# A mixture-of-experts tail on one core: the 7 busiest of 15 routed experts stay dense, the other 8 run on 64 gathered tokens in fp32 in two column groups

## The reference

```python
E = 16; K = 4                      # 16 routed experts, 4 for each token; D = 512, H = 1365
gate_out = x @ gate_w + routing_bias
top_v, top_i = jax.lax.top_k(gate_out, K)
chosen = jax.nn.one_hot(top_i, E, dtype=x.dtype).sum(axis=-2)
weights = jax.nn.softmax(jnp.where(chosen > 0, gate_out, NEG), axis=-1) * chosen
out = _swiglu(x, sw1, sw2, sw3)    # the shared expert
for e in range(E):
    out = out + _swiglu(x, w1[e], w2[e], w3[e]) * weights[..., e:e + 1]
# _swiglu(x, w1, w2, w3): a = x @ w1; return a * sigmoid(a) * (x @ w2) @ w3
```

## Time and profile before

| | before |
|---|---|
| time, median of 3 | 535.69 us |
| the profiled execution | 535.71 us |
| its span | 533.7 us |
| mean granted TensorE clock | 0.994 |
| PE busy | 522.6 us |
| DVE busy | 425.1 us |
| ACT busy | 337.2 us |
| moved by DMA | 190.11 MB |

### The profile page before, as it was taken

The page is one execution under the profiler, slowest core; times in us unless marked ns, Lnnn a source line. Parts: engine busy times, 40 slices in busy tenths (PEclk is TensorE's granted clock), DMA queues, the critical chain, the costliest instruction groups (busy, mean ns, idle before and its releaser), DMA issues.

```text
span 533.7 us, 7582 instructions
## 1 busy us (share of the span) xinstructions
PE 522.6 (98%) x2672; PEld 406.9 (76%) x2672; DVE 425.1 (80%) x426; ACT 337.2 (63%) x324; POOL 8.9 (2%) x40
## 2 busy tenths in 40 slices
PE   8999799999999999999999999999999999999998
PEld 4665335467878888888888888888888888888886
DVE  6724610167899989889898998989998988989796
ACT  1100100158787878788786877877787877778573
POOL 2000000011000000000000000000000000000000
PEclk9988999999999999999999999999999999999999
DMA  8999999999999999999989999899999999999331
GB/s 338 422 421 421 421 421 422 417 409 416 414 404 414 372 375 348 351 394 337 404 284 380 374 344 384 320 381 339 368 358 356 345 341 395 340 369 350 123 108 70
DMA packets 37032, 190.11 MB, mean 356 GB/s; under 512 B 4090, under 2 KB 4474, under 8 KB 31636
## 3 DMA queue, kind: packets, MB, share of 16 engines
q1 hardware_dynamic: 36816, 189.70, 92.0%
q10 hardware_dynamic: 196, 0.14, 0.1%
HBM read 189.56 MB, written 0.26 MB: 356 GB/s over the span
## 4 chain that ended last, share of the span: by engine, by line
PE 91%; DVE 7%; ACT 1%; issue 1%; DMA 1%; POOL 0%; DVEq 0%; ACTq 0%; POOLq 0%
PE ps L1572 29%; PE ps L1610 23%; PE ps L1576 14%; PE ps L1594 4%; PE ps L1221 3%; PE ps L1385 3%; DVE s_lo L891 2%; PE ps L1414 1%; PE ps L1402 1%; PE ps L1214 1%; PE ps L1283 1%; PE ps L1299 1%; DVE s_lo L903 1%; PE ps L1273 1%; PE ps L1287 1%; PE ps L1545 1%
## 5 line engine op out<-in xcount | busy, mean ns | idle before, releaser
L891 DVE TENSOR_TENSOR s_lo<-w_raw,s_hi 128x1365 fp32r<-128x1365 f32 x136 | 209.1, 1579 | 16.0 <-ACT s_hi L657 15.6
L657 ACT CAST s_hi<-w_raw 128x1365 fp32r<-128x1365 f32 x136 | 180.4, 1337 | 26.3 <-PE ps L1576 13.1
L1572 PE MATMUL ps<-s_hi,xT_hi 128*128 128x512 f32 (+1 forms) x408 | 153.7, 377 | 0.3 <-DVE s_lo L891 0.3
L1572 PE MATMUL ps<-s_lo,xT_hi 128*128 128x512 f32 (+1 forms) x408 | 149.7, 369 | 0.0
L1576 PE MATMUL ps<-s_hi,xT_lo 128*128 128x512 f32 (+1 forms) x408 | 106.6, 369 | 0.0
L903 DVE TENSOR_TENSOR s_lo<-w_raw,s_hi 128x1536 fp32r<-128x1536 f32 x68 | 105.8, 1578 | 0.0
L669 ACT CAST s_hi<-w_raw 128x1536 fp32r<-128x1536 f32 x68 | 90.8, 1343 | 21.4 <-PE ps L1576 18.3
L1572 PEld LDWEIGHTS ps<-s_hi,xT_hi 128*128 128x128 f32 x408 | 76.6, 188 | 17.0 <-DVE s_lo L891 0.5
L1572 PEld LDWEIGHTS ps<-s_lo,xT_hi 128*128 128x128 f32 x408 | 77.0, 189 | 12.5
L1576 PEld LDWEIGHTS ps<-s_hi,xT_lo 128*128 128x128 f32 x408 | 72.7, 189 | 6.0
L1610 PE MATMUL ps<-s_hi,hT_hi 128*128 128x512 f32 (+1 forms) x180 | 72.8, 404 | 0.2 <-DVE hT_lo L1097 0.2
(11 more groups left out here) (249 smaller groups left out, 305.5 us busy)
## 6 DMA issues: line engine op xcount, KB each, us to landing
w_raw<-in_w SPq DMA_DIRECT2D x128, 682.5 KB, 6.2
w_raw<-in_w SPq DMA_DIRECT2D x51, 768.0 KB, 6.1
w_set<-in_w SPq DMA_DIRECT2D x31, 1024.0 KB, 24.5
w_raw<-in_w SPq DMA_DIRECT2D x12, 512.0 KB, 5.8
w_raw<-in_sw SPq DMA_DIRECT2D x8, 682.5 KB, 15.6
wk_sb<-in_wk SPq DMA_DIRECT2D x2, 1024.0 KB, 16.6
wq_sb<-in_wq SPq DMA_DIRECT2D x2, 1024.0 KB, 16.0
gcn_sb<-in_gcn_w SPq DMA_DIRECT2D x2, 1024.0 KB, 13.1
```

The source lines that it names most:

```text
L657: a.copy(s_hi[pair][:, 0:F1], raw[:]).then_inc(hi_ready, 1)
L891: v.tensor_tensor(s_lo[pair][:, 0:F1], raw[:], s_hi[pair][:, 0:F1].bitcast(F32), ALU.subtract).then_inc(lo_ready, 1)
L1572: mm(bank(i + c0 // D)[:, 0:n], xT_hi[:, k], w[:, c0:c0 + n], start=(k == 0 and w is hi), stop=False)
```

## The change

Routed expert 0 stays at its place as a dense body. The other 15 are sorted on the chip by how many tokens chose them. Since 128 tokens choose 4 each, at most 7 experts can have more than 64 tokens. The 7 busiest run densely as before (bodies D), the other 8 as sparse bodies (S), in the order `KINDS`:

- A 0/1 matrix `hots` picks the tokens of each sparse expert: four matmuls gather x into `exS`, 64 rows an expert (`gather_few`). `spread`, made of the gates, later adds the 64 rows of the result back to the 128 (`spread_few`, `add_few`).
- A sparse body multiplies the raw fp32 weights as they are, without a split. The 64 tokens take 64 of the 128 columns of the array; the other 64 get the same tokens and the second half of the expert's 1365 features (683 each). A raw tile is free again when TensorE has used it (`raw_used`).
- SyncE reads each body's expert number from a table made by `plan_order`, and waits for that table before the loads of body 2.
- There are five pairs instead of six, all loops are written out, and w3 is laid out by single experts (dense: 11 tiles each; sparse: the two halves, 6 tiles each, the last of 43 rows).

```diff
-JOIN = 3
-JOINED = NE // JOIN * JOIN - (NE % JOIN == 0) * JOIN
-assert NE - JOINED == 2
-ALONE = JOIN
-CARRY = [F1 * j // P * P for j in range(1, JOIN)]
-CARRY = [0] + [F1 * j - c for j, c in zip(range(1, JOIN), CARRY)] + [0]
-TILES = [(F1 + CARRY[j]) // P for j in range(JOIN - 1)] + [-(-(F1 + CARRY[JOIN - 1]) // P), FT]
-LAST_ROWS = [P] * (JOIN - 1) + [F1 + CARRY[JOIN - 1] - (TILES[JOIN - 1] - 1) * P, F1 - (FT - 1) * P]
-H_COLS = max(FT * P, F1 + max(CARRY))
-DOWN = [[(0, 3), (3, 3), (6, 3), (9, n - 9)] for n in TILES]
-HT_CHUNK = [[(0, 4), (4, 4), (8, n - 8)] for n in TILES]
-W3_UNITS = len(DOWN[0])
-UNITS = 2 * KT + W3_UNITS
+LAST_ROWS = F1 - (FT - 1) * P
+DOWN = [(0, 3), (3, 3), (6, 3), (9, FT - 9)]
+HT_CHUNK = [(0, 4), (4, 4), (8, FT - 8)]
+W3_UNITS = len(DOWN)
+FEW = P // 2
+HALVES = P // FEW
+CW = -(-F1 // HALVES)
+S_TILES = -(-CW // P)
+S_LAST = CW - (S_TILES - 1) * P
+S_LOADED = -(-S_LAST // 16) * 16
+S_CHUNK = [(0, 512), (512, CW - 512)]
+S_HT = [(0, 4), (4, S_TILES - 4)]
+BUSY = P * K1 // (FEW + 1)
+KINDS = "DD" + "SD" * 5 + "SSDSD"
+FULL = [m for m in range(NE) if KINDS[m] == "D"]
+SPARSE = [m for m in range(NE) if KINDS[m] == "S"]
...
-PAIRS_N = 6
+PAIRS_N = 5
...
+    unit_of, few_of = {}, {}
+    for m in range(NE + 1):
+        for part, e, n in ((0, m, KT), (2, m - 1, W3_UNITS), (1, m, KT)):
+            if 0 <= e < NE:
+                numbers = unit_of if KINDS[e] == "D" else few_of
+                for k in range(n):
+                    numbers[e, part, k] = len(numbers)
...
+            def wait_unused(m, part, k):
+
+                if is_full(m):
+                    sp.wait_ge(lo_ready, unit_of[m, part, k] + 1)
+                else:
+                    sp.wait_ge(raw_used, few_of[m, part, k] + 1)
...
+            next_up(1, 0, w1[0])
+            next_up(1, 1, w2[0])
+            sp.wait_ge(table_ready, 1)
+            expert_now, expert_then = None, None
+            for m in range(2, NE):
+                at = FULL.index(m) - 2 if is_full(m) else BUSY + SPARSE.index(m)
+                expert_now = sp.value_load(table[0:1, at:at + 1], min_val=1, max_val=E1 - 1)
+                next_up(m, 0, one(w1, expert_now))
+                if m == 2:
+                    for u in range(W3_UNITS):
+                        wait_unused(0, 2, u)
+                        load_down(w3[1], u)
+                else:
+                    next_down(m - 1, expert_then)
+                next_up(m, 1, one(w2, expert_now))
+                expert_then = expert_now
+            next_down(NE - 1, expert_then)
...
+            def silu_few(e):
+
+                act.wait_ge(raw_used, few_of[e, 0, KT - 1] + 1)
+                act.wait_ge(h_ready, e)
+                a.activation(act_a[:, 0:CW], few_row(0), ACT.Silu).then_inc(act_ready, 1)
...
+            def gated_few(e):
+
+                dve.wait_ge(act_ready, e + 1)
+                dve.wait_ge(raw_used, few_of[e, 1, KT - 1] + 1)
+                dve.wait_ge(hT_ps, turned(e))
+                rows = hS[:].rearrange("p t n -> p (t n)")[:, 0:CW]
+                v.tensor_tensor(rows, act_a[:, 0:CW], few_row(NC), ALU.mult).then_inc(h_ready, 1)
+
+            def copy_y(e):
+
+                dve.wait_ge(raw_used, few_of[e, 2, W3_UNITS - 1] + 1)
+                if few_no(e) > 0:
+                    dve.wait_ge(added, few_no(e))
+                v.tensor_copy(y_sb[:], bank(7)).then_inc(y_few_ready, 1)
...
+            def plan_order():
+
+                dve.wait_ge(counts_ps, 1)
+                v.tensor_copy(table_in[:], bank(7)[:, 0:2 * E1].rearrange("p (a e) -> p a e", a=2)).then_inc(counts_ready, 1)
+                dve.wait_ge(counts_ready, 1)
+                pairs = [P, E1, E1]
+                then(v.scalar_tensor_tensor(order_key[:], counts, float(E1), iota[:, 0:E1], ALU.mult, ALU.subtract))
+                then(v.memset(order_key[:, 0:1], float(-P)))
+                then(v.tensor_tensor(ahead[:], order_key[:].unsqueeze(1).to_broadcast(pairs),
+                                     order_key[:].unsqueeze(2).to_broadcast(pairs), ALU.is_gt))
+                then(v.tensor_reduce(place_no[:], ahead[:], AX_X, ALU.add))
+                places = [P, E1 - 1, E1]
+                then(v.tensor_tensor(at_place[:], iota[:, 0:E1 - 1].unsqueeze(2).to_broadcast(places),
+                                     place_no[:].unsqueeze(1).to_broadcast(places), ALU.is_equal))
+                then(v.tensor_tensor(scratch[:], at_place[:], iota[:, 0:E1].unsqueeze(1).to_broadcast(places), ALU.mult))
+                then(v.tensor_reduce(expert_at[:], scratch[:], AX_X, ALU.add))
+                v.tensor_copy(table[:], expert_at[:]).then_inc(table_ready, 1)
...
+            for m in range(2, NE):
+                if is_full(m):
+                    lo_w1(m, 0)
+                    lo_w1(m, 1)
+                    gated_few(m - 1)
+                    lo_w1(m, 2)
+                    lo_w1(m, 3)
+                    lo_w2(m, 0)
+                    copy_y(m - 1)
+                    for k in range(1, KT):
+                        lo_w2(m, k)
+                elif is_full(m - 1):
...
+            def up_few(e, part, k):
+
+                pe.wait_ge(ld_up[part][k], 16 * (e + 1))
+                w = (w1_raw, w2_raw)[part][k]
+                tokens = slice(FEW * few_no(e), FEW * few_no(e) + FEW)
+                for c0, n in S_CHUNK:
+                    for g in range(HALVES):
+                        last = mm(bank(NC * part + c0 // D)[FEW * g:FEW * g + FEW, 0:n], exS[:, k, tokens],
+                                  w[:, CW * g + c0:CW * g + c0 + n], start=(k == 0), stop=(k == KT - 1), skip_group_check=True)
+                last.then_inc(raw_used, 1)
...
+            def down_few(e, u):
+
+                pe.wait_ge(ld_down[u], down_loads(e, u))
+                if u == 0:
+                    pe.wait_ge(y_few_ready, few_no(e)) if few_no(e) > 0 else pe.wait_ge(round_ready, KT + 2)
+                for i in range(3 * u, 3 * u + 3):
+                    t, g = i // HALVES, i % HALVES
+                    if g == 0 and t in (0, KT) or i == 0:
+                        pe.wait_ge(hTS_ready, len(S_HT) * few_no(e) + t // KT + 1)
+                    rows, own = P if t < S_TILES - 1 else S_LAST, slice(FEW * g, FEW * g + FEW)
+                    last = mm(bank(7)[own], hTS[0:rows, t, own], w3_raw[0:rows, i], start=(t == 0), stop=(t == S_TILES - 1),
+                              skip_group_check=True)
+                last.then_inc(raw_used, 1)
...
+            def add_few(e):
+                pe.wait_ge(y_few_ready, few_no(e) + 1)
+                mm(bank(6), spread[:, few_no(e)], y_sb[:], start=False, stop=False, skip_group_check=True).then_inc(added, 1)
...
+            for m in range(NE):
+                up_part(m, 0, 0)
+                up_part(m, 0, 1)
+                if m == 1:
+                    count_chosen()
+                if m == 2:
+                    spread_few(1)
+                if m > 0:
+                    transpose_h(m - 1, 0)
+                up_part(m, 0, 2)
+                if m > 0:
+                    transpose_h(m - 1, 1)
+                up_part(m, 0, 3)
+                if m > 0 and is_full(m - 1):
+                    transpose_h(m - 1, 2)
+                for u in range(W3_UNITS if m > 0 else 0):
+                    if is_full(m - 1):
+                        down(m - 1, u)
+                    else:
+                        down_few(m - 1, u)
+                    if m == 1 and u > 0:
+                        gather_few(u - 1)
                 for k in range(KT):
-                    up_w2(e, k)
-
-            body(1, kind_of(0))
-            with pe.Fori(2, JOINED - 1, JOIN) as e0:
-                for j in range(JOIN):
-                    body(e0 + j, (j + 1) % JOIN)
-            for e in range(JOINED - 1, NE - 1):
-                body(e, kind_of(e - 1))
+                    up_part(m, 1, k)
+                    if m == 1 and k == 0:
+                        gather_few(KT - 1)
+                    if m == 1 and k == 2:
+                        spread_few(0)
+                    if m == 2 and k == 0:
+                        pe.wait_ge(round_ready, KT)
+                    if k == 1 and m > 0 and not is_full(m - 1):
+                        add_few(m - 1)```

**Order on TensorE, a dense body behind a sparse one** (body 3 of the change). In these rows `w_raw` are raw weight tiles, `exS` the gathered tokens, `hS` and `hTS` the sparse h and its transpose. Before, between the last w1 unit and the first w2 unit of a body stood:

```order
L1594 MATMUL ps<-ident,h 128x128 x3
L1599 ISA
L1605 ISA
L1610 MATMUL ps<-s_hi_84,hT_hi 128x512
L1610 MATMUL ps<-s_lo_90,hT_hi 128x512
L1610 MATMUL ps<-s_hi_84,hT_lo 128x512
```

More of the change, by code:

```diff
@@ L562, in _ @@
             pool.wait_ge(q_ps, 2)
-            clear_pads(range(4, 5))
-            pool.wait_ge(gnn1_ps, 1)
-            clear_pads(range(5, PAIRS_N))
+            clear_pads(range(4, PAIRS_N))
```

(68 more changed lines are left out.)

501 lines of the change are left out of this document (248 added, 253 removed).

## The result

The time fell from 535.72 us (median of 4 runs, 535.51 to 536.18) to 529.07 (529.03 to 531.01): a ratio of 0.9884, 95% interval 0.986 to 0.9907. That is 6.7 us of the 29 forecast, and outside the range. The profiled execution, the longest of the four, took 531.01 us for a span of 529.2.

A forecast was written before the change was run, and what follows sets the result against it. TensorE was taken to bound at 23.78 us an expert, DVE and weight stream close behind. First stretch to 182.1 plus 321.8 for 15 experts gave span 503.9; 2.0 around it made 506, 1 for the stream 507 us; range 496 to 524.

The forecast's parts named there:

- second spread 0.9: Among the remaining 15 experts on PE from 182.1: the second spread adds 0.9 us.
- a shortfall of up to 1 us a pair over seven pairs mostly stays in that slack. I add 1 us: Weight stream over pairs of bodies: queue runs dry about 1 us a pair, mostly absorbed; 506 becomes 507 us.
- 5 to 12 us before PE wants it: Weight loads in the pair followed through: each lands this long before PE needs it.
- three round trips: PE switches between column groups and full width where one sparse body follows another: three, at 0.30 us each.
- (a): Rival, steady state: stream bounds below its burst rate, a pair takes 44.6 us, 3.3 more than PE; 522 us, chance 0.18.
- the 3.4 us in the table: Measured over forecast: bodies 3 to 10, 167.8 against 165.6 us; bodies 11 to 13, 59.4 against 58.2.
- the 2.5 at the end: Body 16 and the end: forecast 36.4 us, measured 38.9, difference +2.5.
- (c): Rival, sparse bodies on PE: column groups don't overlap, 14.3 us more for each of eight; 620 us, chance 0.03.
- it costs nothing unless the stream bounds: Table wait before the third body's loads: queue dry some 5 us while PE has 30 us of work; no cost.
- the 0.30 taken from the earlier trace: PE's switch between column groups and full width, in and out: 0.30 us a trip, 38 trips, 11.4 us.

The follow-up runs named there:

- experts 1 and 4 alone: Against the kernel with ScalarE's spread copy later and the two sparse bodies in a row at 2 and 3: h ahead of w3 subtractions in these experts; 516.83 us.
- Half the columns: Against the changed kernel: sparse bodies load 683 of the 1365 columns of w1 and w2, with the same PE work; 521.22 us.
- fixed expert numbers: Against the changed kernel: SyncE neither waits for the table nor reads it, body m takes expert m-1; 528.95 us.
- Late copy and half columns: Against the changed kernel: ScalarE's second spread copy behind the third w3 copy, and sparse bodies load 683 of 1365 columns of w1 and w2; 513.86 us.
- the late copy: Against the changed kernel: ScalarE's second spread copy moved from the start of body 2 to behind the third w3 copy; 520.30 us.

## Why the prediction was wrong

**First failing step: body 2 "second spread 0.9".** The second spread was costed on PE alone, 0.9, and its copy on ScalarE not at all. For a gather the sum has both ScalarE's copy (0.5) and the conversion that stands behind it; of the second spread I did not ask what is queued behind its copy. It holds ScalarE until PE has done two units of body 2 and the spread, behind it stand the w3 copies of expert 1, behind these two subtractions and h, and PE needs h at once. Price forecast 0, measured 8.3 us in the body (30.0 to 21.7) and 8.8 in the time. The remaining 1.5 us over 20.2 are the wait for h of 1.68 us, behind two w3 subtractions: with h ahead of them (experts 1 and 4 alone) the body took 20.0.

**Second failing step: "a shortfall of up to 1 us a pair over seven pairs mostly stays in that slack. I add 1 us".** The rate was right: 391 to 402 GB/s at a share of 1.00 to 1.02 from 213 to 440, against the 398 taken from the earlier trace rows. Two things in that step were wrong. One is the slack "5 to 12 us before PE wants it". That was counted for w1 and w2. The tight load is w3 of a dense expert: its tile is free only after the sparse down-projection, some 11 us into the dense body, and after its landing come a copy, two subtractions and h. The copy of its first unit (L721 on ScalarE's timeline) began 17.3, 18.0, 18.5, 18.7 and 18.8 us into the dense bodies 3 to 11 of the changed kernel. Behind body 5 h was ready at 279.93 and PE wanted it at 280.5 (278.0 and two up units of 1.23): half a microsecond of slack, and two pairs on, behind body 9, it was used up (a wait of 0.24). The other is the two sparse bodies in a row, which I priced on PE (three round trips) and never against the stream: bodies 12 and 13 take PE 36.7 us and load 16.8 MB, 42 us at 400 GB/s. Behind them that copy began 23.8 us into body 14, 5.0 later than before. Half the columns took it back to 16.4 and the wait to nothing. Price forecast 1, measured 7.9 us (529.07 to 521.22); of the 7.8 at body 15, 5.25 are the wait, and 2.5 the clock that fell behind it, where the forecast has it at 1.00.

So of the rivals (a) came nearest in place, the stream, but not in mechanism: it named a rate of 378 GB/s and a loss in each pair. Its time, 522, lies 7 us under the measured one, because the larger stall was in none of the cases.

**Sizes that were off.** A dense body took 22.8 us, not 22.1, and the excess is spread over its joints, between up units and transposes and around the y copy; I did not take it apart further. Over bodies 3 to 13 that is nearly all of the 3.4 us in the table. Of the 2.5 at the end, 0.7 are the same excess in body 16, and some 1.5 lie in the last down-projection, where the granted clock was 0.50 from 517.43 to 520.84, after waits of 1.79 and 0.94 us; in the profiled runs where it stayed at 1.00, with the same two waits, body 16 and the end took 37.4 us. When that down-projection starts was forecast well: 4.15 us after the last up unit (513.06 to 517.21), 4.0 forecast.

**What held.** hT_lo of the second chunk ended at 164.0 (163.8 forecast), body 2 began at 183.43 (182.1). That is no luck of two errors: `plan_order` took 3.0 us (3.0) and `plan_tokens` 3.4 (3.3). What the forecast did not have there is PE's wait of 4.06 us at 153.05, behind `plan_order`, with the granted clock at 0.50 from 152.20 to 159.03. It cost nothing that can be seen, because VectorE is the path there. A sparse body took 19.1 to 19.4 us (19.3), four up units in a row 4.76, 1.19 each (1.14), and a down-projection 5.30 to 5.47 with its switch (5.15 + 0.30). The column groups run side by side, so (c) is out.

In the timeline of body 4 above, from start to start, a transpose group takes 0.59 us where it took 0.44, and a unit 1.30 where four in a row take 1.19 each: 0.15 + 0.11, some 0.26 a round trip, against the 0.30 taken from the earlier trace rows. And "it costs nothing unless the stream bounds", of the bend at the table, held (fixed expert numbers) even though the stream did bound later: the raw tiles fill up and the lead is lost.

**The sum with both stalls out.** Late copy and half columns gave 513.86, against 507 forecast. Its profiled run (span 512.7) lies over the forecast span of 503.9 by 1.6 us ahead of body 2, 1.5 in it, 3.2 in bodies 3 to 15 and 2.4 from body 16 on, 8.8 in all. Less the 1 added for the stream, 0.3 around the span and 0.6 between this run and the median, these are the 6.9 us between the times. The sum on PE was right to 1.5%; the two large misses are an order and a load.

**What stays open.** Behind the late copy, four further arrangements gave 516.6 to 517.6 with intervals that overlap. Each shortened the wait aimed at, and a wait for a load of the same kind, or for hT_lo instead of h, stood in its place or in a later body. That the stream sets this level is likely (the share is 1.01 to 1.02 throughout, and half the columns lies 3 us below), but not shown. How much of the wait at body 15 varies between executions (4.80 and 2.89 us with the same loads) and why the clock fell after some short waits and not after others isn't settled either. No run gave w3 a second buffer or another place in SyncE's order, so whether that ends the late landings is not known; nor was the step from six pairs to five tried by itself (40.1 of the 45.2 us that L721 waited ended with a load, so there is little room for it).

## What to carry to other kernels

When work is added on one engine, follow each copy that it needs on the other engines, and ask what stands behind that copy in that engine's order: 0.59 us of ScalarE cost 8.8 us. When a change makes compute as short as the stream, don't set averages against each other; find the load with the latest release and the longest tail behind its landing, write down its slack in the trace of before, and check each irregular stretch of the schedule (here two cheap bodies in a row) for bytes against time. Once both are full, reordering mostly moves waits (behind the late copy the best order gave 3.7 us, 520.30 to 516.57, though it ended more than that in waits): price an order by the time of the whole, not by the wait that it ends. And add to a long wait what the clock costs behind it.
